# Layer 1's two weight products made of seven quarter products in place of eight, in a two-layer graph network on one Trainium2 core

## What is computed

```python
# x (64, 256, 512), adj (64, 256, 256)
# layer 0
h = jnp.maximum(_layernorm(x, axis=-1), 0.0)
query, keyt, value = h @ Wq.T + bq, h @ Wk.T + bk, h @ Wv.T + bv
weight = adj * jnp.exp(query @ keyt.T)
x = x + (weight / weight.sum(axis=2, keepdims=True)) @ value
# layer 1
h = jnp.maximum(_layernorm(x, axis=-1), 0.0)
deg = jnp.sum(adj, axis=-1, keepdims=True)
agg = jnp.einsum('bij,bjf->bif', adj, h) / jnp.maximum(deg, EPS)
x = x + relu(jnp.concatenate([h, agg], axis=2) @ W1.T)      # W1 (512, 1024)
```

## Time and profile before

| what | value |
|---|---|
| median of 3 runs | 1982.36 us (1981.8 to 1982.73) |
| the profiled execution, its time | 1980.83 us |
| its span, first to last instruction | 1979.0 us |
| busy in the span | PE 1965.9 us (99%), DVE 1316.7 (67%), POOL 902.5 (46%), ACT 777.9 (39%) |
| granted TensorE clock | 1.00 of full speed |
| one step of the loop | 60.68 us |
| DMA | 236.47 MB, 119 GB/s over the span |

### The profile page before, as it was taken

One profiled execution on the slowest core, in us unless ns is written; L12 is line 12 of the kernel. 1 busy time (PEld: TensorE's weight loads), 2 busy tenths in 40 slices (PEclk: granted clock), 3 DMA queues, 4 the chain that ended last, 5 costly groups with the idle time before them and its releaser, 6 DMA issues.

```text
span 1979.0 us, 28170 instructions
## 1 busy us (share of the span) xinstructions
PE 1965.9 (99%) x9356; PEld 1649.3 (83%) x9356; DVE 1316.7 (67%) x2331; ACT 777.9 (39%) x1289; POOL 902.5 (46%) x956
## 2 busy tenths in 40 slices
PE   8999999999999999999999999999999999999999
PEld 5888888888888888888888888888888888888887
DVE  6777667766667666677666676666766666766654
ACT  4434344333443343443434433444434344333432
POOL 2545454445445354444444453545445444445440
PEclk9999999999999999999999999999999999999999
DMA  5243333333433324324333334333343333333421
GB/s 193 100 145 101 131 128 107 131 118 115 132 114 114 138 96 137 132 101 138 117 117 127 117 117 135 98 132 124 108 144 103 131 127 108 126 121 112 132 70 43
DMA packets 162370, 236.47 MB, mean 119 GB/s; under 512 B 14769, under 2 KB 111025, under 8 KB 162353
## 3 DMA queue, kind: packets, MB, share of 16 engines
q1 hardware_dynamic: 162352, 236.25, 35.7%
HBM read 137.63 MB, written 98.57 MB: 119 GB/s over the span
## 4 chain that ended last, share of the span: by engine, by line
PE 98%; DVE 1%; issue 0%; DMA 0%; ACT 0%; SPq 0%
PE bank L364 32%; PE bank L365 32%; PE bank L366 32%; PE bank L509 0%; PE bank L510 0%; DMA x_in<-x 0%; DVE w L819 0%; DVE h L804 0%; DVE stats L768 0%; PE bank L372 0%; DVE n_l L744 0%; ACT wv_h L590 0%; ACT wb_h L590 0%; SPq L218 0%; SPq L217 0%
## 5 line engine op out<-in xcount | busy, mean ns | idle before, releaser
L304 POOL TENSOR_TENSOR gT_l<-turned,gT_h 128x512 fp32r<-128x512 f32 x124 | 173.2, 1418 | 372.2 <-ACT gT_h L609 372.1
L304 POOL TENSOR_TENSOR hT_l<-turned,hT_h 128x512 fp32r<-128x512 f32 x122 | 178.8, 1486 | 188.1 <-ACT hT_h L578 188.1
L880 DVE SCALAR_TENSOR_TENSOR y<-bank,deg_inv,y 128x512 f32<-128x512 f32 x128 | 96.1, 751 | 214.0 <-PE bank L366 212.7
L748 DVE STREAM_TRANSPOSE blocks<-h 128x512 f32<-128x512 f32 x248 | 161.3, 688 | 109.7 <-DMA turned_store<-blocks 84.4
L618 ACT ACTIVATE y<-bank 128x512 f32<-128x512 f32 x128 | 76.6, 599 | 324.9 <-PE bank L366 324.9
L364 PE MATMUL bank<-hT_h,n_h 128*128 128x512 f32 x512 | 199.5, 390 | 3.4 <-DVE bqk L840 1.8
L364 PE MATMUL bank<-wv_h,hT_h 128*128 128x512 f32 x512 | 199.6, 390 | 0.0
L365 PE MATMUL bank<-wv_l,hT_h 128*128 128x512 f32 x512 | 199.6, 390 | 0.0
L365 PE MATMUL bank<-hT_l,n_h 128*128 128x512 f32 x512 | 199.2, 389 | 0.0
L366 PE MATMUL bank<-hT_h,n_l 128*128 128x512 f32 x512 | 199.2, 389 | 0.0
L366 PE MATMUL bank<-wv_h,hT_l 128*128 128x512 f32 x512 | 199.2, 389 | 0.0
(11 more groups left out here) (126 smaller groups left out, 4708.3 us busy)
## 6 DMA issues: line engine op xcount, KB each, us to landing
turned_store<-blocks SPq DMA_DIRECT2D x124, 512.0 KB, 3.4
turned<-turned_store SPq DMA_DIRECT2D x496, 128.0 KB, 2.8
x_in<-x SPq DMA_DIRECT2D x32, 1024.0 KB, 5.3
out<-x SPq DMA_DIRECT2D x124, 256.0 KB, 2.0
adjT<-adj_t SPq DMA_DIRECT2D x32, 512.0 KB, 3.5
w<-adj SPq DMA_DIRECT2D x32, 512.0 KB, 4.8
x<-wq SPq DMA_DIRECT2D x4, 256.0 KB, 3.6
xb<-wk SPq DMA_DIRECT2D x4, 256.0 KB, 3.9
```

The lines of the kernel that those rows point to most:

```text
L304: pool.tensor_tensor(by_blocks(dst, t), turned_tile(t), by_blocks(high, t).bitcast(F32), ALU.subtract).then_inc(done, 1)
L748: nc.vector.transpose(blocks[:, :, :, t % NT, :].rearrange("p j c b -> p c j b"), h[:, t, :].rearrange("p (c j b) -> p c j b", c=DT, b=Q)) ...
L880: nc.vector.scalar_tensor_tensor(out=y[:, :], in0=bank[L1_BANK + 1][:, :], scalar=deg_inv[:, t:t + 1], in1=y[:, :], op0=ALU.mult, op1=ALU. ...
```

## The change

h of a pair is cut in quarters A11, A12 (first graph, features 0 to 255 and 256 to 511) and A21, A22 (second graph), and [W1b | W1a] in B11, B21 (W1b, upper and lower half of the features) and B12, B22 (W1a). With S1 = A21 + A22, S2 = S1 - A11, S3 = A11 - A21, S4 = A12 - S2 and T1 = B12 - B11, T2 = B22 - T1, T3 = B22 - B12, T4 = B21 - T2 the four results are sums of seven products of 256 x 256 by 256 x 512:

- z of graph 0 = A11 B11 + A12 B21
- U2 = A11 B11 + S2 T2, U3 = U2 + S3 T3
- z of graph 1 = U3 + A22 T4
- ha of graph 1 = U3 + S1 T1
- ha of graph 0 = U2 + S1 T1 + S4 B22

A product is two rounds r (128 rows of the quarter) of 6 matmuls of 512 columns. The sums with U are made in PSUM as far as they follow each other (banks X: A11 B11, then S2 T2, S3 T3 and A22 T4 on top; banks Z: S1 T1, then S4 B22 on top); ACT copies banks X out at three points (`copy_p0`, `copy_u2`, `copy_u3`), and DVE adds (`sum_z`, `sum_ha1`, `sum_ha0`). S1 to S4 are made in each step by DVE (`combine_...`) from `turned`, split by ACT (`high_part`) and POOL (`low_part`). T1 to T4 are made once, in step 0, by POOL. The split T1 and T2 find no place in SBUF: they are kept in DRAM, and in each step loaded over n_h and n_l after the key products (`load_t`), and n_h and n_l are loaded anew after S2 T2 (`load_n`), 2 MB each. The last pair's h now takes the road through DRAM too.

The diff, cut to the loop's step:

```diff
+A11, A12, S1, S3, S2, A22, S4 = range(1, 8)
+B11, B21, T3, T1, T2, T4, B22 = range(1, 8)
+PRODUCTS = (A11, A12, S1, S2, S3, A22, S4)
+WEIGHTS = (B11, B21, T1, T2, T3, T4, B22)
+ROUNDS = 2
+PER_PAIR = len(PRODUCTS) * ROUNDS
+X_BANK, Y_BANK, Z_BANK = (4, 2), (5, 6), (7, 3)
...
+            def load_t(i):
+                sp.wait_ge(kp_psum, DT * (i + 1))
+                sp.dma_start(n_h[:, :, :].bitcast(F32), t_d[0]).then_inc(t_loaded, 16)
+                sp.dma_start(n_l[:, :, :].bitcast(F32), t_d[1]).then_inc(t_loaded, 16)
+
+            def load_n(j):
+                sp.wait_ge(p_psum, PER_PAIR * j + products_done(3, 1))
+                sp.dma_start(n_h[:, :, :].bitcast(F32), n_d[0]).then_inc(n_loaded, 16)
+                sp.dma_start(n_l[:, :, :].bitcast(F32), n_d[1]).then_inc(n_loaded, 16)
...
+            def low_part(j, m):
+                pool.wait_ge(part_high, 7 * j + m)
+                pool.tensor_tensor(part_blocks(part_l[m]), part_source(m), part_blocks(part_h[m]).bitcast(F32),
+                                   ALU.subtract).then_inc(part_split, 1)
...
-                def z(t):
-                    if layer0:
-                        pe.wait_ge(gT_split, T * j + t + 1)
-                    elif t == 0:
-                        pe.wait_ge(last_split, DT)
-                    if t == 0 and first:
-                        pe.wait_ge(weight_split, PIECES)
-                    if t >= 2:
-                        pe.wait_ge(z_split, T * j + t - 1)
-                    elif not first:
-                        pe.wait_ge((ha_copied, y_done)[t], T * j)
...
-                def layer1_products(t):
-
-                    g, it = divmod(t, NT)
-                    if t == 0:
...
+            def strassen(j, p, r):
+                part, weight = PRODUCTS[p], WEIGHTS[p]
+                dst = {0: X_BANK, 1: Y_BANK, 2: Z_BANK, 3: X_BANK, 4: X_BANK, 5: X_BANK, 6: Z_BANK}[p][r]
+                rows = [slice(c * ROUNDS * P + r * P, c * ROUNDS * P + (r + 1) * P) for c in range(2)]
+                product(bank[dst][:, :],
+                        [(part_h[part][:, rows[c]], part_l[part][:, rows[c]], mix_h[weight][:, c, :], mix_l[weight][:, c, :])
+                         for c in range(2)], start=p < 3, more=p in (3, 4, 5, 6)).then_inc(p_psum, 1)
...
+                pe.wait_ge(part_split, 7 * j + A11)
+                if is_first(i):
+                    pe.wait_ge(mix_split, T2)
+                    pe.wait_ge(b22_split, 1)
+                strassen(j, 0, 0)
+                strassen(j, 0, 1)
+                pe.wait_ge(part_split, 7 * j + A12)
+                strassen(j, 1, 0)
+                strassen(j, 1, 1)
+                pe.wait_ge(part_split, 7 * j + S1)
+                pe.wait_ge(t_loaded, 32 * i)
+                pe.wait_ge(v_split, T * i + 2)
+                strassen(j, 2, 0)
+                strassen(j, 2, 1)
+                pe.wait_ge(part_split, 7 * j + S2)
+                pe.wait_ge(p0_copied, ROUNDS * j + 1)
+                strassen(j, 3, 0)
+                pe.wait_ge(p0_copied, ROUNDS * j + 2)
+                strassen(j, 3, 1)
+                pe.wait_ge(at_split, j + 1)
+                pe.wait_ge(z_split, T * j + NT)
+                pe.wait_ge(v_split, T * (i + 1))
+                az(j, 0, AZ_BANK[0])
+                pe.wait_ge(u2_copied, ROUNDS * j + 1)
+                strassen(j, 4, 0)
+                pe.wait_ge(u2_copied, ROUNDS * j + 2)
+                strassen(j, 4, 1)
+                az(j, 1, AZ_BANK[1])
+                pe.wait_ge(part_split, 7 * j + A22)
+                if is_first(i):
+                    pe.wait_ge(mix_split, T4)
+                pe.wait_ge(u3_copied, ROUNDS * j + 1)
+                strassen(j, 5, 0)
+                pe.wait_ge(u3_copied, ROUNDS * j + 2)
+                strassen(j, 5, 1)
+                pe.wait_ge(part_split, 7 * j + S4)
+                pe.wait_ge(ha1_done, ROUNDS * j + 1)
+                strassen(j, 6, 0)
+                pe.wait_ge(ha1_done, ROUNDS * j + 2)
+                strassen(j, 6, 1)
+                pe.wait_ge(z_split, T * (j + 1))
+                az(j, 2, AZ_BANK[2])
+                az(j, 3, AZ_BANK[3])
+                pe.wait_ge(ha0_done, ROUNDS * j + 1)
+                sum_weights(i, SUM_BANK)
+                pe.wait_ge(ha0_done, ROUNDS * j + 2)
+                av(i, 0, AV_BANK[0])
+                pe.wait_ge(y_done, T * j + 1)
+                av(i, 1, AV_BANK[1])
+                pe.wait_ge(y_done, T * j + 2)
+                av(i, 2, AV_BANK[2])
+                pe.wait_ge(y_done, T * j + 3)
+                av(i, 3, AV_BANK[3])
...
+            def copy_p0(j, r):
+                act.wait_ge(p_psum, PER_PAIR * j + products_done(0, r))
+                nc.scalar.activation(z_sum[r], bank[X_BANK[r]][:, :], ACT.Copy).then_inc(p0_copied, 1)
+
+            def copy_u3(j, r):
+                act.wait_ge(p_psum, PER_PAIR * j + products_done(4, r))
+                nc.scalar.activation(ha1[r], bank[X_BANK[r]][:, :], ACT.Copy).then_inc(u3_copied, 1)
+
+            def copy_u2(j, r):
+                act.wait_ge(p_psum, PER_PAIR * j + products_done(3, r))
+                nc.scalar.activation(u2[r], bank[X_BANK[r]][:, :], ACT.Copy).then_inc(u2_copied, 1)
...
+                high_v(i, 3)
+                act.wait_ge(combined, 4 * j + 1)
+                high_part(j, S1)
+                act.wait_ge(sum_psum, i)
+                copy_p0(j, 0)
+                act.wait_ge(combined, 4 * j + 2)
+                high_part(j, S3)
+                copy_p0(j, 1)
+                act.wait_ge(combined, 4 * j + 3)
+                high_part(j, S2)
+                high_part(j, A22)
+                high_z(j, 0)
+                high_z(j, 1)
+                act.wait_ge(combined, 4 * j + 4)
+                act.wait_ge(p_psum, PER_PAIR * j + products_done(0, 1))
+                high_part(j, S4)
+                copy_u2(j, 0)
+                copy_u2(j, 1)
+                act.wait_ge(z_split, T * j + NT)
+                high_sum(i)
+                act.wait_ge(sum_split, i + 1)
+                copy_u3(j, 0)
+                copy_u3(j, 1)
...
+            def combine(dst, a, b, op):
+                nc.vector.tensor_tensor(dst, a, b, op).then_inc(combined, 1)
+            def combine_s1(j):
+                dve.wait_ge(g_moved[1], 64 * (j + 1))
+                combine(staged(), quarter(1, 0), quarter(1, 1), ALU.add)
+            def combine_s3(j):
+                dve.wait_ge(combined, 4 * j + 1)
+                combine(quarter(1, 0), quarter(0, 0), quarter(1, 0), ALU.subtract)
+            def combine_s2(j):
+                dve.wait_ge(part_split, 7 * j + S1)
+                combine(staged(), staged(), quarter(0, 0), ALU.subtract)
+            def combine_s4(j):
+                dve.wait_ge(part_split, 7 * j + S2)
+                combine(staged(), quarter(0, 1), staged(), ALU.subtract)
+            def sum_z(j, r):
+                dve.wait_ge(p_psum, PER_PAIR * j + products_done(1, r))
+                dve.wait_ge(p0_copied, ROUNDS * j + r + 1)
+                nc.vector.tensor_tensor(z_sum[r], bank[Y_BANK[r]][:, :], z_sum[r], ALU.add).then_inc(z_summed, 1)
+            def low_z(j, t):
+                g, r = divmod(t, NT)
+                low(kz_l[:, t, :], z_sum[r] if g == 0 else bank[X_BANK[r]][:, :], kz_h[:, t, :], z_high, T * j + t + 1, z_split)
+            def sum_ha1(j, r):
+                dve.wait_ge(u3_copied, ROUNDS * j + r + 1)
+                nc.vector.tensor_tensor(ha1[r], bank[Z_BANK[r]][:, :], ha1[r], ALU.add).then_inc(ha1_done, 1)
+            def sum_ha0(j, r):
+                dve.wait_ge(p_psum, PER_PAIR * j + products_done(6, r))
+                dve.wait_ge(u2_copied, ROUNDS * j + r + 1)
+                nc.vector.tensor_tensor(u2[r], bank[Z_BANK[r]][:, :], u2[r], ALU.add).then_inc(ha0_done, 1)
...
+                low_v(i, 1)
+                if not is_first(i):
+                    dve.wait_ge(x2_done, T * j)
+                combine_s1(j)
+                combine_s3(j)
+                low_v(i, 2)
+                low_v(i, 3)
+                combine_s2(j)
+                sum_z(j, 0)
+                sum_z(j, 1)
+                low_z(j, 0)
+                combine_s4(j)
+                low_z(j, 1)
+                dve.wait_ge(h_done[0], T * (i + 1) + NT)
+                dve.wait_ge(g_stored[1], 16 * (j + 1))
+                turn(0, h_turned)
+                dve.wait_ge(part_split, 7 * j + S4)
+                turn(1, h_turned)
+                key_bias_of(i + 1, 0)
+                turn_h(i + 1, 1)
+                sum_ha1(j, 0)
+                sum_ha1(j, 1)
+                key_bias_of(i + 1, 1)
+                key_bias_of(i + 1, 2)
+                low_z(j, 2)
+                key_bias_of(i + 1, 3)
+                low_z(j, 3)
...
```

1282 lines of the change are left out of this document (749 added, 533 removed).

## The result

The changed kernel takes 1993.32 us (median of 4 runs, 1991.2 to 1994.64) where the kernel before takes 1982.34: a ratio of 1.0054, 95% interval 1.0042 to 1.0066. The forecast was 1905, range 1893 to 1950. It is wrong by 88 us and on the wrong side.

What follows compares the result with a forecast made beforehand. PE, busy 99%, was taken as the bound; twelve fewer matmuls a step gave 58.2 us, 2.48 saved. 30 x 2.48 = 74.4, + 2.7 + 1.5 - 1.0 = 77.6 off 1980.8: 1903.2, median 1905, range 1893 to 1950.

Steps and rivals of the forecast that it cites:

- The chain to the next h, steps 1 to 3: From PE's v(3) at 27.54 us into a loop step: low parts of S1 at 30.35, S2 33.2 to 34.6, S4 38.3 to 39.6.
- X: Time in a loop step when S4's low part is done: 38.3 to 40.6 us forecast, with margin up to 39.75.
- What eats the margin: DVE and POOL locking each other out, and DVE starting the next loop step late, given 0 to 1 us on X.
- step 3: S4's link of the chain: low part done at 38.3 to 39.6 us, upper value with one collision each for S2 and S4.
- Both legs fit: After E, DVE's work and n's reload both end before PE wants them, the reload by 0.2 to 1.5 us.
- The reload's leg: From E to n_h and n_l landed: E + 13.5, 56.5 to 57.8 us; PE wants it at 57.96.
- E: Time in a loop step when the next h is out of DVE: X + 4.7, 43.0 to 44.3 us.
- DVE's leg: DVE's ha sums, key biases and kz_l after E: done at 47.9 to 49.2 us; PE wants the last at 49.30.
- Ends: Setup and the last two loop steps: +1 us for setup (bounds -1 to +5), -2.7 and -1.5 for those two.
- The reload's rival: n's two loads don't overlap and land at E + 16.1: 59.1 to 60.4 us a step, 1949 us in all; chance 0.09.
- the locks' rival: DVE and POOL locks delay S1, S3, S2, A22: X 41.5 to 43, 59.7 to 60.6 us a step, 1946 to 1975 in all; 0.10.
- slower: Dearer combinations, low parts and more locks push X past 42.5; at 43.2, 61.4 us a step, 2002 in all; chance 0.08.

Runs made afterwards that it cites:

- e10: Changed kernel with S1's low part moved on POOL ahead of the second graph's low weights and row sums: 2044.7 us, ratio 1.0314.
- e13: Changed kernel reordered: S1's parts first, S2 ahead of S3, S4's combination and h's first transpose ahead of the two kz_l: 1962.8 us, ratio 0.9899.
- e1: Changed kernel without the reload of n_h and n_l, so layer 0 is not the reference's: 1953.5 us.
- e8: Changed kernel with S2 ahead of S3 on all engines, and ACT's second copy of P0 ahead of S2's high part: 2017.6 us, ratio 1.0167.
- e3: Changed kernel without the output stores in the loop and without DVE's wait for them: 1955.6 us.
- e9: Changed kernel with layer 1's results in other tiles, so DVE doesn't wait for the output stores, which stay: 2003.3 us, ratio 1.0118.
- e6: Changed kernel with the output stores issued on ACT's queue in place of SyncE's: 2031.0 us, ratio 1.0238.
- e5: Changed kernel with neither n's reload nor the loop's output stores (edits of e1 and e3 together): 1967.6 us.
- e12: Changed kernel with n's second load in four column blocks, a semaphore each, on the same queue: 2025.8 us, ratio 1.0218.
- e15: e13 with both kz_l ahead of h's first transpose, their high parts ahead of S4's, and the last step's degrees behind its combinations: 1969.9 us, ratio 0.9934.

## Why the prediction was wrong, point by point

Against the forecast of 1903 for the profiled execution 91 us are missing: 67 in the 29 steps of the loop (60.5 in place of 58.2), 5 in step 1, 5 in setup and 14 behind the loop.

**What is taken from PE: right.** 230 matmuls 0.227 apart, 57.96 of work in a step, and the 60.64 above adds up from it.

**The chain to the next h, steps 1 to 3: late from the first link.** The prediction started the chain at PE's v(3) and gave S1's low part 30.35; it was 32.7 in the step shown, 32.4 in the median. It asked when the data are there, and not what stands ahead of them on engines that work in order. POOL has w_l, scales, A11, A12, scales, w_l and the row sums from u = 20.4 to 30.9 without a gap; ACT holds v(3)'s high part and S1's behind h's tiles 2 and 3, for which it waits on scales from that same POOL. Neither is enough by itself: moving S1 on POOL alone lost 51 us (e10), moving it on both and S2, S4's combination and h's transpose with it brought 30 (e13). The prediction had POOL's idle half as its argument against such a loss; the idle half lies elsewhere (10.2 us in a piece before 942.60). What this lateness costs is set by S2: forecast for 34.6 at the latest and wanted at 35.70, it came at 36.2; in e1, where nothing else holds the step, it came at 36.6, and the step is 36.6 + 22.6 = 59.2. That X still came out at 40.5, inside the forecast's 38.3 to 40.6, is partly luck: the allowances for locks and for DVE's late start covered a delay of another kind.

**What eats the margin: half right.** The locks were there on S2's and S4's combinations, 1.1 each, which the upper value of step 3 held. e8 took one of them away and won nothing, but it also put S3's combination in front of S4's, so it does not price a lock by itself. From X on the prediction's X + 4.7 held (4.8).

**"Both legs fit": the step that failed.** The reload's leg was E + 13.5, from 5.1 for 2.1 MB at the 410 GB/s of a moment in which x was loaded beside one store of blocks. It was 15.2. 0.5 of the difference is between E and the store of h's second half, from which the prediction's 5.3 and 7.9 were counted (967.80, 968.28). The other 1.2 is the output's megabyte, which the prediction left out on this queue: without it n_l takes 7.8 and the leg is 14.0 (e3), with it 9.0, and 9.3 to 10.2 in e8, e9 and e6. The windows of the changed kernel, just before the step's end, show less than 410 (columns from the clock on: granted clock, DMA share, GB/s):

```profile
978.00:980.00 2.00, 2.00 (x11) 1.65 (x10) 1.93 (x4) 0.00 (x0) 2.00 (x2) 1.00 1.03 307
980.00:982.90 2.90, 1.44 (x7) 0.86 (x5) 2.44 (x3) 0.00 (x0) 1.96 (x1) 1.00 0.91 323
```

So a step is not max(57.96, X + 18.2) but X + 4.8 + 15.2: with the median X of 40.5, 60.5. These are parts of the measured step put together again, not a check of it. The forecast's 58.2 stands for X = 40.0, so 1.8 of the 2.3 that a step is too long come from this leg and 0.5 from X. DVE's leg held: PE has no wait before az(2).

**Why it is a cycle.** A late n delays the key products, these the scores, these POOL's first weights, and with them S1, S4, h and n again. e1 and e3 each remove one piece and bring 1.25; both together (e5) no more, because S2 is next. e12 loosens the landing and the wait goes elsewhere. e13 shortens the chain up to X by 2.2, up to E by 1.1 (two kz_l now stand between) and the step by 1.2, and PE still starts with n's landing; e15 makes E 0.5 later and the step 0.4 longer.

**DVE's late start: 8.0 after the step's start, forecast 5.5 to 7.0.** 1.15 of it is the wait for output stores,'s 6.06 had none; the prediction listed DVE's operations and not what they wait for. e9, without that wait, has 7.0, and its step is no shorter, so in the changed kernel this start holds nothing. It can: in e12, where it is 10.7, all of the chain is 3 us later.

**Ends: +1.0 forecast for setup, +6.2 measured; -4.2 for the last two steps, +9.8 measured.** In setup nine POOL operations of 2.4 to 3.5 stand beside DVE's work, and some of them hold it:

```profile
52.28 4.11 DVE L1151 TENSOR_TENSOR w<-w,adjT 128x512 f32<-128x512 f32 x2
56.31 2.88 DVE L237 TENSOR_TENSOR w_l<-w,w_h 128x512 fp32r<-128x512 f32 x1
...
59.56 0.68 DVE L237 TENSOR_TENSOR w_l<-w,w_h 128x512 fp32r<-128x512 f32 x1
```

2.88 and 0.68 are the same operation with and without POOL's mixing beside it; PE then waits 3.2 for the row sums (0.53 in the kernel before). At the end the last step's first DVE operation waits for adj, whose load stands behind the output stores, and all combinations stand behind it:

```profile
1956.32 1.22 DVE L1092 TENSOR_REDUCE deg<-w 128x4 f32<-128x1024 f32 x1 [4.19 <-DMA w<-adj]
...
1957.87 0.68 DVE L1157 TENSOR_TENSOR y<-turned 128x512 f32<-128x512 f32 x1
```

so PE waits 7.6 for S1's low part where 1.2, for S2's, was priced. In e15, with the degrees behind the combinations, that wait is 1.9, but the next one, for kz_l, is 5.0: kz_l now stands behind S1, S2, S4 and the degrees. The stretch is 1.5 shorter. What a better place for the degrees would bring is not shown.

**The clock was not in the sum at all.** Before, the granted clock is 1.00 until the last 3 us. After, it falls to 0.50 twice in setup, once in the loop (behind a wait of 1.86 for n at 194.59) and three times at the end. Setup, in windows of PE (busy, clock, DMA share, GB/s):

```profile
24.00:26.00 2.00, 1.52 (x10) 0.81 0.00 0
26.00:28.00 2.00, 2.00 (x11) 0.50 0.00 0
28.00:30.00 2.00, 1.82 (x5) 0.50 0.39 102
```

Added up over all windows of 2 us, (1 - clock) x 2 is 13.7 us after and 0.6 before. Some of that lies over waits and beyond the last instruction, so it is an upper bound of what the low clock cost; 12 of it fall on the ends, which lost 16. How the 16 divide into waits and clock was not tested.

**The rivals.** The reload's rival came nearest: it had E + 16.1 and a step of 59.1 to 60.4. Of the locks' rival hardly anything came beyond the two that the forecast's own upper X held; its upper X of 43 also does not go with its 60.6 (43 + 18.2 is 61.2, and 60.6 is X = 42.4). What stood under "slower" (X past 42.5, 0.08) was another road; the changed kernel's X stays under 41.3, e12's is 43.5, with a step of 61.7. The chance for slower was far too low because the 0.2 to 1.5 us of margin in the reload's leg was taken as covering every unknown at once: an in-order queue, a store behind the load, and a lock.

**Open.** Why T's load is later in e5; why e8's n_l takes 9.9 with its stores on the same queue as in the changed kernel; and how the 57.96 could be reached: the best step, 59.44, still waits 0.9 for kz_l.

## What to carry to other kernels

Taking work from the bound engine pays only as far as the next cycle is short, and that cycle runs through engines that are half idle: list, for each link, what stands ahead of it in its engine's own order, and not only when its data are there. In such a kernel try the order early: the same operations in another order were worth 30 us (1.5%) here, not much less than leaving out n's reload (40) or the output stores (38) altogether. But move the whole chain: one move alone (e8, e10) made it slower. Price a load together with the stores that follow it: here their megabyte made the second megabyte of n 1.2 us longer, half of the 2.3 by which a step is too long. And a wait that vanishes from the list has not always left the cycle: look whether the engine still starts with the same release.

## What the runs showed of the hardware that was not expected

- A load is slowed by stores issued after it: 7.8 us for the second megabyte of n with nothing behind it (e3), 9.0 with four stores of 256 KB behind it, the last issued just as it lands (the changed kernel), 9.3 and 9.9 in e9 and e8, also on its own queue, 10.2 with the stores on another (e6).
- A wait of PE costs 0.27 to 0.30 more than the idle time in its row, at full clock (0.16 ahead of it, the rest over the next twelve matmuls).
- The granted clock fell to 1.2 GHz after waits of 1.81 and 1.86 us (24.48 and 194.59 in the changed kernel) and not after others of 0.8 to 1.76 in each step, nor after one of 1.83 in the kernel before. The wait's length alone doesn't decide: in e6 one of 3.16 (at 627.3) left the clock at 1.00, one of 2.87 (at 933.6) was followed by some 6 us at 1.2 GHz.
- DVE's two-operand operations beside a POOL instruction end some 0.55 after it: 1.75 for 0.68 beside one of 1.28, 2.88 for 0.68 beside one of 2.72.
